# Causal attention and a routed expert layer on one core: the transpose of a head's maxima moved behind the next chunk's scores, in the same PSUM bank

## The reference, cut

```python
x = x + _layernorm(attn(_layernorm(x)))     # x: 8 x 1024 x 256, 16 heads of 16
x = x + _layernorm(ffn(_layernorm(x)))      # 8 experts of 512, the top 2 of each row

def attn(x, Wq, Wk, Wv, Wo):
    q, k, v = (heads(x @ W.T) for W in (Wq, Wk, Wv))       # b h n d
    score = einsum('bhnd,bhmd->bhnm', q, k) / 4            # 1024 x 1024 for each of 128 heads
    score = where(causal, score, -inf)
    out = einsum('bhnm,bhmd->bhnd', softmax(score), v)
    return out.transpose(0, 2, 1, 3).reshape(B, S, D) @ Wo.T
```

## Time and profile before

| what | us |
|---|---|
| median of 3 runs | 2004.83 (2004.69 to 2005.61) |
| the profiled execution, its time | 2003.3 |
| its span, first to last instruction | 2001.5 |
| PE busy | 1863.6 (93%) |
| DVE busy | 1589.5 (79%) |
| ACT busy | 1324.0 (66%) |
| POOL busy | 934.5 (47%) |
| pass of the maxima, first copy to last copy of `mrow` | 65.7 to 1141.8 |
| transposes (L1393) and copies (L804) | 128 each |

### The profile page before, as it was taken

The page is one execution under the profiler, slowest core; times in us unless marked ns, Lnnn a source line. Parts: engine busy times, 40 slices in busy tenths (PEclk is TensorE's granted clock), DMA queues, the critical chain, the costliest instruction groups (busy, mean ns, idle before and its releaser), DMA issues.

```text
span 2001.5 us, 76386 instructions
## 1 busy us (share of the span) xinstructions
PE 1863.6 (93%) x26830; PEld 1283.6 (64%) x26831; DVE 1589.5 (79%) x5285; ACT 1324.0 (66%) x3387; POOL 934.5 (47%) x1439
## 2 busy tenths in 40 slices
PE   6799999999999999999999899999999999999980
PEld 3244555455555455455444359899999999999980
DVE  3888888888888888888888748778777777777767
ACT  5277788878888888888777775554444444544436
POOL 4333344456656566565555654554323333333335
PEclk9799999999999999999999999999999999999995
DMA  6734656475555646464547378889889989898848
GB/s 204 212 119 128 192 170 207 150 217 167 184 168 162 191 146 201 139 190 154 169 145 232 109 231 259 238 248 261 257 258 261 263 259 263 261 267 243 244 121 338
DMA packets 257628, 411.79 MB, mean 206 GB/s; under 512 B 36912, under 2 KB 194352, under 8 KB 250160
## 3 DMA queue, kind: packets, MB, share of 16 engines
q1 hardware_dynamic: 217856, 363.46, 56.3%
q0 software_dynamic: 29680, 35.41, 9.5%
q10 hardware_dynamic: 9792, 8.93, 1.5%
HBM read 284.83 MB, written 122.28 MB: 203 GB/s over the span
## 4 chain that ended last, share of the span: by engine, by line
PE 81%; DVE 9%; issue 4%; ACT 3%; DMA 2%; SPq 1%; POOL 0%; DVEq 0%; ACTq 0%; POOLq 0%
PE ps_s L1540 18%; PE ps_o L1424 11%; PE ps_s L1372 10%; PE ps_w L1372 10%; PE ps_e L1372 10%; PE ps_e L1540 6%; PE ps_e L1557 6%; PE ps_o L1557 6%; DVE cmax L797 3%; DVE arena L794 2%; PE ps_e L1550 1%; DVE space L128 1%; ACT arena L1164 1%; PE ps_w L1500 1%; PE ps_w L1437 1%
## 5 line engine op out<-in xcount | busy, mean ns | idle before, releaser
L1164 ACT ACTIVATE arena<-ps_e 128x512 f32<-128x512 f32 (+3 forms) x1536 | 686.4, 496 | 211.2 <-PE ps_e L1372 204.0
L1372 PE MATMUL ps_s<-arena 96*32 96x512 bf16 (+3 forms) x6144 | 506.6, 334 | 31.8 <-DVE mrow L804 12.5
L1372 PE MATMUL ps_e<-arena 98*32 98x512 bf16 (+3 forms) x6144 | 517.8, 330 | 10.6 <-ACT arena L1164 8.3
L797 DVE TENSOR_REDUCE cmax<-ps_s 128x1 f32<-128x512 f32 x512 | 338.0, 680 | 21.7 <-PE ps_s L1372 20.4
L1372 PEld LDWEIGHTS ps_s<-arena 96*32 96x32 bf16 x6144 | 173.9, 96 | 219.5 <-DVE rmax L794 101.1
L794 DVE CUSTOM_DVE_ANT_0 arena<-ps_s,c,cmax 128x128 bf16<-128x128 f32 (+3 forms) x512 | 268.1, 541 | 51.3 <-PE ps_s L1372 46.1
L1424 PE MATMUL ps_o<-arena 128*32 128x512 f32 (+3 forms) x3072 | 296.4, 487 | 3.4 <-ACT ot L1178 2.8
L794 DVE CUSTOM_DVE_ANT_0 arena<-ps_s,c 128x128 bf16<-128x128 f32 (+3 forms) x512 | 234.0, 491 | 61.7 <-PE ps_s L1372 58.7
L669 POOL DMA_INDIRECT acc<-blank,place_now x135 | 213.1, 1578 | 142.0 <-DMA acc<-blank,place_now 63.9
L1372 PEld LDWEIGHTS ps_e<-arena 98*32 98x32 bf16 x6144 | 175.3, 97 | 155.8 <-issue 54.9
L686 POOL TENSOR_SCALAR_AFFINE_SELECT arena<-arena 128x512 f32<-128x512 f32 x256 | 162.6, 635 | 241.1 <-ACT arena L1164 240.4
(11 more groups left out here) (182 smaller groups left out, 2983.8 us busy)
## 6 DMA issues: line engine op xcount, KB each, us to landing
arena<-in_gate_up SPq DMA_DIRECT2D x91, 1024.0 KB, 5.9
arena<-qk_parts SPq DMA_DIRECT2D x384, 128.0 KB, 3.0
c_h<-in_gate_up SPq DMA_DIRECT2D x44, 1024.0 KB
qk_parts<-space SPq DMA_DIRECT2D x120, 192.0 KB
d_xin<-xs SPq DMA_DIRECT2D x136, 130.5 KB, 3.2
arena<-v_aug SPq DMA_DIRECT2D x32, 512.0 KB, 6.0
o_t<-ot SPq DMA_DIRECT2D x64, 256.0 KB, 2.6
v_aug<-space SPq DMA_DIRECT2D x28, 512.0 KB, 5.3
```

The source lines that it names most:

```text
L797: dve.reduce_max(cmax[:, par, i - NB:i - NB + 1], ps_s[:, m % RS, 0:w], AX.X).then_inc(s_cmax, 1)
L1164: act.activation(pw[:, at % RP, begin:end], ps_e[:, n % RE, 0:w], ACT.Exp, scale=SCALE).then_inc(e_done, 1)
L1372: last = pe.matmul(out[at:at + QUAD], lhsT[:, at:at + QUAD], rhs, start=start, stop=stop)
```

## The change

The transpose is issued one chunk later, ahead of chunk 8's scores and not behind chunk 7's, and it writes the last 64 float32 columns of bank 2, beside the 256 columns of chunk 8 and not in their place. DVE copies it behind the maximum of chunk 8. Chunk 8's scores no longer wait for the copy; chunk 11's, the next ones in bank 2, do. The transpose still waits for `s_mlo` and for the maximum of chunk 5. The numbers of instructions and their sizes stay the same. ACT's and POOL's lists are unchanged.

```diff
-    ROWS_AT, HIGH_AT = 7, 3
+    ROWS_AT, HIGH_AT = 8, 3
...
-        rows_tile = ps_s[0:2 * SB, RS - 1, 0:P // 2].bitcast(BF16)
+        rows_tile = ps_s[0:2 * SB, ROWS_AT % RS, HALF - P // 2:HALF].bitcast(BF16)
...
+                    if 0 <= m < HEADS * NM:
+                        maximum(m)
                     if 0 <= m < HEADS * NM + NM and m % NM == ROWS_AT and m >= NM:
                         max_rows(m // NM - 1)
-                    if 0 <= m < HEADS * NM:
-                        maximum(m)
...
-                if c == ROWS_AT + 1 and head >= 1:
+                if c == ROWS_AT + RS and head >= 1:
                     pe.wait_ge(rows_sb, head)
...
-                pe.wait_ge(s_cmax, min((n + 1) * NM + ROWS_AT + 2 - RS, HEADS * NM))
+                pe.wait_ge(s_cmax, min((n + 1) * NM + ROWS_AT + 1 - RS, HEADS * NM))
...
+                    if NM <= m < HEADS * NM + NM and m % NM == ROWS_AT:
+                        max_rows(m // NM - 1)
                     if 0 <= m < HEADS * NM:
                         max_scores(m)
-                    if NM <= m < HEADS * NM + NM and m % NM == ROWS_AT:
-                        max_rows(m // NM - 1)
```

## The result

| what | before | after |
|---|---|---|
| median, beside each other, us | 2004.76 (2000.06 to 2005.61, 4 runs) | 1987.9 (1984.88 to 1990.88, 4 runs) |
| ratio, 95% interval | | 0.9922 [0.9908, 0.9935] |
| profiled execution, its time / span, us | 2003.3 / 2001.5 | 1990.88 / 1989.1 |

The account below looks back on a forecast made before the run. TensorE's order of work was taken to set the pace, with DVE or ACT able to hold it up. 35 waits x 0.38 = 13.3 us off 2003.3 gives 1990.0, plus 1.5 makes 1991.5 us; range 1984 to 2004.

Parts of the forecast that it names:

- The mechanism at head 3: Transpose at head 3 no longer waits for DVE's maximum of chunk 5: 0.38 us each, 35 times, 13.3 us.
- Head 0: Chunk 8's 0.54 us wait for the copy only moves to ACT behind chunk 10, 0.93 not 0.39 us: no gain.
- The copy at nothing: Copy behind chunk 8's maximum costs DVE 0.14 us, covered by idle time; chunk 11's wait for it costs nothing.
- The 9 early waits at 0.38 each, 3.4 us: Waits for chunk 5's maximum between 100 and 260 us, at heads 2 and 3, each counted at 0.38 us.
- Head 1. Gain 0: At head 1 nothing waits at the transpose, and DVE does the same work up to chunk 9 reordered: gain 0.
- From 980 on, one wait in each of 4 groups, 1.5 us: Of 14 late waits at the transpose, only one per group counted, since successive ones looked like DVE's own pace.
- The transpose at nothing new: Transpose ahead of chunk 8 costs 0.02 us as before, nothing new; upper bound 0.22 us times 128, +26 us.
- POOL's 42 waits: Between 260 and 980 us, POOL's `mpart` was taken to stop TensorE at the transpose 42 times, 13.1 us.
- its last rival: Change doesn't remove what it says: ruled out except for the `mpart` semaphore, holding the transpose 0.3 us a time; no chance given.
- Given back: Rival: each removed wait brings TensorE sooner to the next late DVE or ACT; 2001 to 2005 us, chance 0.18.
- The wait for the copy counts as well: Rival: head 0's 0.54 us is gained 29 times too, 1975.5 us; chance of gaining over 20 us 0.10.
- The copy leaves DVE's idle time: Rival: copy behind chunk 8 delays maxima of chunks 9 to 11 by 0.14 us; about 2013 us, slower 0.10.

Follow-up runs that it names:

- behind_exponentials: Changed kernel, late copy included, with the transpose one step earlier, behind the scores for the exponentials and ahead of the product with the values: 1993.24 us, ratio 0.9944.
- transpose_late_only: Kernel before, with only the transpose issued behind the scores for the exponentials; columns, copy and chunk 8's wait as before: 1997.66 us, ratio 0.9973.
- xn_moved_before: Kernel before, with ACT's pair of L1272 instructions and the load of its rows moved four slots later: 2008.87 us, ratio 1.0025.
- xn_moved_after: Changed kernel, with ACT's pair of L1272 instructions and the load of its rows moved four slots later: 1990.55 us, ratio 0.9935.
- after_again: The changed kernel run once more, unaltered, as base for the second set: 1986.96 us, ratio 0.9914 to the kernel before.
- Copy_late_only: Changed kernel with the transpose back behind chunk 7's scores, still in its new columns and with the late copy: 1998.28 us, ratio 0.9973.
- copy_twice_2: Changed kernel with DVE's copy of the maxima made a second time, into a tile nobody reads: 2016.44 us, ratio 0.9931.
- after_third: The changed kernel, unaltered, as base for the fourth set: 2004.99 us, ratio 0.9883 to the kernel before.

## Why the prediction was right, and where it was not

**The mechanism at head 3 was right, in place and size.** 0.38 us were forecast for each wait, 0.39 are gone at the place that was looked at, and 34.30 became 33.96 where about 33.95 was forecast; 0.05 us of it were lost again to the transpose, which the forecast had at nothing new. behind_exponentials and transpose_late_only show it from the other side: a place 0.17 us too early leaves 0.17 us of wait and costs 0.17 us a group.

**Head 0 was right.** 0.93 us of waiting for ACT were forecast, 0.92 measured; with the copy late and nothing else, the group keeps its length. xn_moved_before and xn_moved_after show that the cause is ACT's order of work.

**The copy at nothing was right for the regular groups.** The copy follows chunk 8's maximum with no effect on the length of a group; even a second one has none. Chunk 11's wait for it isn't seen in the stretch of 260 to 980 us. It is in the last heads: tile `mrow`, 980 to 1145 us, after, who waited:

```profile
  PE ps_s L1372: 3.3, 6
```

**Three terms of the sum were too small.** The forecast was 13.3 us, and 16.9 came. By the table above, the three stretches gained 17.1 us, and the rest of the run was 2.2 longer.

- *The 9 early waits at 0.38 each, 3.4 us.* A group there took 33.32 us (transposes 135.38 and 168.70 before) and takes 32.39 (137.06 and 169.45 after): 0.93 a group, 0.47 for each of its two waits. Heads 4 to 24 gained 4.6 us (5.0 in after_again). The step that failed is that the wait of one place in the middle was taken for all.
- *"Head 1. Gain 0", and the groups as all alike.* One group looked at stood for all. In every fourth group the copy did hold up chunk 8 at head 1 (0.26 us in the rows above), and that group gained 0.73 us and not 0.34. With 21 x 0.34 and 5 x 0.39 the heads 24 to 108 gain 9.1 us; 9.5 were measured, 8.4 forecast. Copy_late_only, which leaves the wait for chunk 5 in place, gave 1.3 us there.
- *From 980 on, one wait in each of 4 groups, 1.5 us.* DVE's waits at the transpose went from 4.1 us in 14 to 1.3 in 4, and the 20 heads gained 3.0. Copy_late_only alone gained 2.5 there. That two or three waits in a row are DVE's own pace was too cautious: with the late copy 2.5 us went although the waits for chunk 5 stayed, so part of the pace was the chain of transpose, copy and chunk 8 itself.

**The transpose at nothing new** was mis-sized by little. It takes 0.055 us of one of four column groups, which the next matmul on all 128 columns pays at head 2: 0.05 us a group, 1.5 us in 29 groups. Its bound of 0.22 us was far off.

The Trainium skill (TensorEngine Tiling (Array Packing), Key Properties) says that changing the tiling mode drains TensorE. Here no drain shows: three of the four matmuls behind the transpose start 0.02 us after it (625.90, 625.92), and a whole further transpose costs 0.055. Whether a transpose of 16 columns beside sets of 32 is a change of mode, the trace doesn't say; so it shows that this pair has no drain, not that the page is wrong.

**POOL's 42 waits were misread, without effect on the sum.** The prediction named them among what stops TensorE, and weighed 0.3 us a time in its last rival. They are waits of the weight load unit. At head 2 the transpose was on time all the same, and at head 0 it was 0.12 us late by the maximum of chunk 5; ACT behind chunk 10 took that too.

**The rivals.** "Given back" fell: regular groups are shorter by 0.34 of the 0.39 us. "The wait for the copy counts as well" fell for the regular groups; a smaller form of it holds in every fourth group, in the last heads, and with ACT's work split. "The copy leaves DVE's idle time" fell in the regular groups, while copy_twice_2 shows that in the last heads there is no such room. Of the signs given, the idle time at the transpose's line was to fall under 2 us and is 2.8, of which 1.9 are the matmuls'; the others came as said, chunk 8 following within 0.02 us at heads 0, 1 and 3 of the group shown, and at head 2 with the same start.

**What stays open.** What cost 2.2 us in the rest of the run, behind the last maximum, is not settled. That stretch takes 863.0 us before and 865.2 and 865.6 in two profiles of the changed kernel, but between 862.5 and 867.2 in the other kernels that leave ACT's work as it was. In the sets at 2030 us nothing was tried on the cause.

## What to carry to other kernels

A wait in an in-order engine is worth its length only if the next wait behind it doesn't end by another engine's clock; follow the engine on to the next place where it idles before counting. Where two edits are to be weighed, look whether one makes the place for the other: here a small result written beside a chunk, not in its place, moved a wait one turn of the ring back, and only that freed the place at which, in a regular group, the transpose waits for nothing. A share of busy time of 82% is no room: a piece of ACT's work of 1.1 us took its wait along to the slot where it was put, and half of it didn't. And count a wait in every kind of group before multiplying: every fourth one was different here.

## What the runs showed of the hardware

- A small copy out of PSUM (16 x 128 bf16), recorded at 0.21 us, takes 0.13 to 0.14 us of DVE's.
- The same program took 2004 us in two sets and 2030 us in two others (1987 and 2005 changed), with chip number 0 on record for one of each. The timelines of the changed kernel, after_again and after_third, run alike up to about 410 us. From there on most groups of the second are 0.6 to 1.4 us longer, mainly between the chunks 7 and 10 beside the transposes of heads 3 and 0; those in which the expert layer's 36 matmuls stand are not. Its TensorE at one such place:

```profile
452.74 1.24 PE L1424 MATMUL ps_o<-arena 128*32 128x512 f32 x6
...
453.79 0.62 PE L1424 MATMUL ps_o<-arena 128*32 128x512 f32 x2
```

The ratios of the changed kernel in the two kinds of set are 0.9914 and 0.9883, with intervals that touch, so a change of 0.3% should be judged within the set it was measured in.
